# Masked two-precision convolution on TensorE: the four-product form for a second band of rows, with GpSimd in the output path

## What is computed

```python
mask = _predictor_mask(x)                 # mean of 8x8 blocks >= 0.05
x_high = jnp.where(mask, x, EPS)
x_low = jnp.where(mask, EPS, x)
y_high = _conv(_quant_act_uint(x_high, act_scale_high, 8), _quant_weight_per_oc(w_high, 8))
y_low = _conv(_quant_act_uint(x_low, act_scale_low, 4), _quant_weight_per_oc(w_low, 4))
return y_high + y_low
```

## Time and profile before

| | before |
|---|---|
| median of 3 runs | 664.49 us (664.17 to 666.38) |
| the profiled execution: time, and span inside it | 662.33 us, 660.5 us |
| PE busy | 635.5 us (96%), 3714 matmuls |
| DVE busy | 594.5 us (90%), 739 instructions |
| ACT busy | 483.7 us (73%), 491 instructions |
| POOL busy | 10.2 us (2%), 30 instructions |
| granted TensorE clock, mean | 0.996 of full speed |

### The profile page before, as it was taken

How to read it: one execution, slowest core, us unless ns; L and a number is a source line. 1 busy time by engine, 2 the same in 40 slices (tenths; PEclk the granted TensorE clock), 3 DMA queues, 4 the chain that set the end, 5 groups by cost and what they waited for, 6 DMA issues and landing times.

```text
span 660.5 us, 10672 instructions
## 1 busy us (share of the span) xinstructions
PE 635.5 (96%) x3714; PEld 355.9 (54%) x3714; DVE 594.5 (90%) x739; ACT 483.7 (73%) x491; POOL 10.2 (2%) x30
## 2 busy tenths in 40 slices
PE   3779999999999999999999999999999999999996
PEld 1345555555555555555555555555555555555554
DVE  7899999999999999999999999999999999999933
ACT  6768787777777778778777778777877877877442
POOL 3200000000000000000000000000000000000000
PEclk9989999999999999999999999999999999999999
DMA  6245445533435543334543344553343454331122
GB/s 266 97 154 195 162 174 195 194 134 128 182 140 194 194 158 124 163 146 188 194 186 127 132 177 157 194 194 148 122 175 139 194 194 170 124 150 68 72 97 98
DMA packets 14409, 104.07 MB, mean 158 GB/s; under 512 B 1728, under 2 KB 1728, under 8 KB 10432
## 3 DMA queue, kind: packets, MB, share of 16 engines
q1 hardware_dynamic: 14400, 103.95, 41.2%
HBM read 52.56 MB, written 51.38 MB: 157 GB/s over the span
## 4 chain that ended last, share of the span: by engine, by line
PE 95%; ACT 2%; DVE 1%; DMA 1%; issue 0%; DVEq 0%; SPq 0%
PE psum L336 95%; DMA wraw_l<-w_low 1%; ACT rounded_h L450 0%; ACT psum L485 0%; ACT wT_l L467 0%; DVE pooled L619 0%; DVE w_max_l L578 0%; ACT wT_h L467 0%; PE psum L322 0%; DVE ybuf L717 0%; DVEq L63 0%; DVE wq_l L601 0%; DVE wint_l L585 0%; DVE upper L701 0%; DVE wq_l L590 0%
## 5 line engine op out<-in xcount | busy, mean ns | idle before, releaser
L485 ACT ACTIVATE psum<-psum,ratio 128x1344 f32<-128x1344 f32 (+2 forms) x159 | 174.4, 1097 | 131.0 <-PE psum L336 128.3
L336 PE MATMUL psum<-plane_l,wT_l 128*128 128x448 f16 (+1 forms) x1164 | 211.7, 330 | 0.0
L336 PE MATMUL psum<-plane_h,wT_h 128*128 128x448 f16 (+1 forms) x1164 | 209.5, 328 | 0.0
L336 PEld LDWEIGHTS psum<-plane_l,wT_l 128*128 128x128 f16 x1164 | 112.9, 97 | 83.1 <-issue 2.4
L336 PEld LDWEIGHTS psum<-plane_h,wT_h 128*128 128x128 f16 x1164 | 112.0, 96 | 81.3
L717 DVE SCALAR_TENSOR_TENSOR ybuf<-psum,out_scale_h,shared 128x448 f32<-128x448 f32 (+1 forms) x194 | 114.3, 605 | 27.5 <-PE psum L336 20.1
L619 DVE TENSOR_REDUCE pooled<-xbuf 128x49 f32<-128x3136 f32 (+2 forms) x33 | 109.4, 3315 | 0.0
L506 ACT ACTIVATE shared<-psum,bias,out_scale_h 128x448 f32<-128x448 f32 (+1 forms) x128 | 86.2, 674 | 26.4 <-PE psum L336 23.5
L450 ACT ACTIVATE rounded_l<-xbuf,inv_act_l 128x1568 int16<-128x1568 f32 (+1 forms) x64 | 101.7, 1591 | 4.8 <-DMA xbuf<-x 4.8
L450 ACT ACTIVATE rounded_h<-xbuf,inv_act_h 128x1568 int16<-128x1568 f32 (+1 forms) x64 | 101.9, 1594 | 0.0
L336 PE MATMUL psum<-rowsum_l,wT_l 128*128 128x448 f16 (+1 forms) x384 | 86.9, 335 | 2.3 <-ACT wT_l L467 2.3
(11 more groups left out here) (78 smaller groups left out, 340.4 us busy)
## 6 DMA issues: line engine op xcount, KB each, us to landing
xbuf<-x SPq DMA_DIRECT2D x31, 1568.0 KB, 6.5
y<-ybuf SPq DMA_DIRECT2D x32, 896.0 KB, 3.6
y<-ybuf SPq DMA_DIRECT2D x32, 672.0 KB, 3.9
xbuf<-x SPq DMA_DIRECT2D x1, 896.0 KB, 7.9
xbuf<-x SPq DMA_DIRECT2D x1, 672.0 KB, 5.3
wraw_l<-w_low SPq DMA_DIRECT2D x1, 576.0 KB, 4.1
wraw_h<-w_high SPq DMA_DIRECT2D x1, 576.0 KB, 6.2
act_scales<-scales SPq DMA_DIRECT2D x1, 1.0 KB, 1.8
```

The lines of the kernel that those rows point to most:

```text
L336: last = nc.tensor.matmul(out, wT[k][:, mat, :], moving(k, p, band, row, dx), start=(k == "l" and j == 0), stop=(j == len(parts) - 1), ski ...
L485: return nc.scalar.activation(banks, banks, ACT.Identity, scale=ratio[:, 0:1])
```

## The change

`FAST` becomes (1, 3): the second band takes the four-product form too, in 31 of 32 images, with its own `outer` and `inner`. At the output of both fast bands the middle sums leave VectorE. ScalarE copies M2 with scale to a new tile `second` in SBUF, right behind `shared`; GpSimd forms `upper` = `shared` - `second` and `lower` = `shared` + `second`; VectorE waits for each and writes the two rows as before. There is one `second`, one `upper` and one `lower` for both bands. TensorE signals M2 (`s_high_second`) and waits before it next overwrites M2 until `second` has been read. On VectorE the low and high differences of both bands stand before and behind the rows of band 1.

```diff
-    FAST = (3,)
+    FAST = (1, 3)
...
+        second = sb("second", [P, N_MAX], F32)
...
+            def halves(n, band):
+                g = BANDS * n + band
+                pool.wait_ge(s_shared, g + 1)
+                pool.wait_ge(s_second, fast_index(n, band) + 1)
+                if not (early(n) and band == FAST[0]):
+                    pool.wait_ge(s_out, 2 * (g - 2) + 2)
+                for to, op, ready in ((upper, ALU.subtract, s_upper), (lower, ALU.add, s_lower)):
+                    nc.gpsimd.tensor_tensor(to[:, 0:columns(band)], shared[band % 2][:, 0:columns(band)],
+                                            second[:, 0:columns(band)], op).then_inc(ready, 1)
...
                     products("l", p, band, "M1")
+                    if not (early(n) and band == FAST[0]):
+                        pe.wait_ge(s_second, fast_index(n, band))
                     products("l", p, band, "M2").then_inc(s_low_inner, 1)
...
-                    products("h", p, band, "M2")
+                    products("h", p, band, "M2").then_inc(s_high_second, 1)
...
+                if fast(n, band):
+                    act.wait_ge(s_high_second, fast_index(n, band) + 1)
+                    nc.scalar.activation(second[:, 0:columns(band)], psum[:, BANK[band % 2]["M2"], 0:columns(band)],
+                                         ACT.Identity, scale=out_scale["h"][:, 0:1]).then_inc(s_second, 1)
...
-                dve.wait_ge(s_shared, g + 1)
-                dve.wait_ge(s_high, TILES * g + 2)
-                for to, scale, ready in ((upper, neg_out_scale, s_upper), (lower, out_scale["h"], s_lower)):
-                    nc.vector.scalar_tensor_tensor(to[:, 0:columns(band)], tile(band, "M2"), scale[:, 0:1],
-                                                   shared[band % 2][:, 0:columns(band)], ALU.mult, ALU.add
-                                                   ).then_inc(ready, 1)
...
-                out_row(n, p, 1, 0)
                 if ahead > 0:
-                    differences("l", m, mp, 3)
-                out_row(n, p, 1, 1)
+                    for band in FAST:
+                        differences("l", m, mp, band)
+                out_rows(n, p, 1)
                 if ahead > 0:
-                    differences("h", m, mp, 3)
+                    for band in FAST:
+                        differences("h", m, mp, band)
```

More of the change, by code:

```diff
@@ L143, in conv_program @@
         s_diff = {k: sem(f"differences_ready_{k}") for k in "hl"}
+        s_high_second = sem("second_product")
+        s_second = sem("second_ready")
         s_upper = sem("upper_ready")
@@ L312, in _, with body @@
                                     ).then_inc(s_bias, 1)
+            def halves(n, band):
[7 more added lines that the diff above has]
+                                            second[:, 0:columns(band)], op).then_inc(ready, 1)
+            def body(i, p, _):
+                n = 2 * i + p
+                if not first_image(n):
+                    for band in FAST:
+                        halves(n, band)
+            over_images(pool, body)
         @block.tensor
@@ L768, in body @@
                     for k in "lh":
-                        differences(k, m, mp, 3)
+                        for band in FAST:
+                            differences(k, m, mp, band)
                     return
```

## The result

| | before | after |
|---|---|---|
| median of the runs | 664.33 us (662.20 to 666.38, 4 runs) | 709.22 us (707.60 to 709.88, 4 runs) |
| profiled execution | 662.33, span 660.5 | 708.67, span 706.9 |
| period of an image, mean of 29 | 19.52 | 21.06 |

The ratio is 1.069, interval 1.0662 to 1.0717. The granted clock was 0.996 before and 0.991 after. The prediction was 698 in a range of 668 to 740. The direction was right and the size 11 us short; of the two slow mechanisms that it named, not the forecast's but the first rival's took place.

What follows compares the result with a forecast made beforehand. TensorE bounds the kernel before, VectorE after: 18.88 own work + 0.2 + 1.6 of waits = 20.7 us per image, 600.3 over 29 images, +35.9 in all, so 697 profiled and 698 forecast, range 668 to 740.

Steps and rivals of the forecast that it cites:

- the first rival: GpSimd cuts in between two differences and VectorE stands for both additions: period 21.3, 715 to 744 us, chance 0.22.
- TensorE needs less; VectorE becomes the bound: Second band loses 3 of 15 matmuls, low and high: TensorE saves 1.24 us per image, needing 18.33; VectorE needs 18.88.
- VectorE's own work, 18.88: VectorE per image: 18.33 before, less 1.19 for the last band's sums, plus 1.74 for two more pairs of differences.
- ScalarE, and when `second` is ready: Second band's `second` ready 11.2 us after the third band's row 0 starts on VectorE; ScalarE busy about 545 us.
- GpSimd's price, 1.09: One GpSimd addition of 448 elements takes 1.09 us, the middle of estimates 0.64, 1.09 and 1.53.
- VectorE's differences run through and GpSimd starts at 12.49: Second band: GpSimd waits for all four differences, so VectorE's row 1 waits about 1.6 us; chance 0.58.
- the row at 16.03: Start-up row: a 62-element GpSimd operation under two VectorE differences took 0.60, not 0.32, ending 0.11 after the second.
- the first band's wait: VectorE's wait for `shared` of the first band, put at about 0.2 us per image.
- they cost nothing: The last band's middle sums fall under block sums and output rows and cost nothing, up to 1.15 a piece.
- Faster without disturbance: Rival: GpSimd starts at 11.2 undisturbed; period 19.4 at 1.09 per addition, about 655 us at 0.95; chance 0.17.
- No change: Rival: VectorE's gain in spare time and its new waits just cancel, period 19.5; chance 0.03.

Runs made afterwards that it cites:

- the run at 634.51: Changed kernel with block sums split ahead of the second and last bands' rows, differences behind the second band's rows, ScalarE reordered so `second` comes earlier: 634.51 us.
- the run without GpSimd: Kernel before with four products in both bands, VectorE forming all middle sums from PSUM and nothing copied to `second`: 703.27 us, ratio 1.0595.
- the run with two copies: Changed kernel with two copies of 128 columns on ScalarE ahead of the second band's `second`, shifting GpSimd's start by about 0.4 us: 699.92 us.

## Why the prediction was right in sign and wrong in mechanism

- **TensorE needs less; VectorE becomes the bound.** Right. The chain has VectorE in front, TensorE is idle 2.4 us in the image shown (2.3 foretold), and the run at 634.51 shows that it gets by with a period of 18.61 and 18.53 busy, where 18.33 was foretold.
- **VectorE's own work, 18.88.** Too big: 18.52 by the run without GpSimd. Most of the difference is in how were read: an idle time counts from the end of the instruction before, but instructions without a wait start about 0.09 before that end. At the three waits in the earlier trace rows I took own work to run to the end and not to the next possible start, 3 x 0.09 = 0.27. That error was against the change, and it also hid how much a good order would bring.
- **ScalarE, and when `second` is ready.** Right: 11.2 on the clock that starts with the third band's first row. In the image shown that row starts at 305.28 and GpSimd at 316.45, 11.17 later; the differences begin at 316.02, 10.74 (10.75 foretold). ScalarE's total was 526 and not 545 because of how the forecast counted: added up one by one, its instructions take 60.6 us more than before, as foretold (2.05 times 30), but the busy time counts once what overlaps, and the overlap of neighbours grew from 24.8 to 42.8 us.
- **GpSimd's price, 1.09.** Right: an addition is recorded with 1.13, and from the start of an undisturbed `upper` to that of `lower` 1.08 to 1.09 pass.
- **The step that failed: "VectorE's differences run through and GpSimd starts at 12.49".** Of the 30 images in which work for a next image follows, three went that way (`upper` at 83.84, 127.03 and 673.19, lasting 2.61 to 2.65 while all four differences kept 0.64 and 0.40). In the first, VectorE's row 1 begins at 87.63; without a wait it would have begun at 85.97 (85.06 and the 0.32 and 0.59 that the last difference and row 0 take from start to start), so it is 1.66 late, against the 1.6 of the forecast:

```profile
83.84 2.61 POOL L326 TENSOR_TENSOR upper<-shared,second 128x448 f32<-128x448 f32 x1 [9.22 <-ACT second L537]
...
85.06 0.40 DVE L711 TENSOR_TENSOR inner_l<-plane_l 128x480 f16<-128x480 f16 x1
...
87.63 0.68 DVE L731 SCALAR_TENSOR_TENSOR ybuf<-psum,neg_out_scale,lower 128x448 f32<-128x448 f32 x1 [0.47 <-POOL lower L326]
```

  In the other 27 GpSimd got in, as the first rival had it. I had set the row at 16.03 of the earlier trace rows above it: one case with a small operation, and the three images show that such cases exist. A single row was no ground for 0.58 against 0.22.
- **The size nevertheless came near**, because both mechanisms charge VectorE about the same (1.88 stood inside two differences, against a wait of 1.6), and by luck: own work was put 0.36 too high, the first band's wait and the threshold together 0.50 too low. To check, the image of 21.10 us adds up as 18.52 own work + 1.88 held + 0.54 at the first band's row (the 0.45 shown and the 0.09 of overlap; 0.2 was foretold) + 0.16 by which the threshold is held under the last band's additions (the next row starts 0.36 behind it, 0.20 in the run without GpSimd) = 21.10. The forecast had 18.88 + 0.2 + 1.6 = 20.7. Over 29 images, 610.84 against 600.3 gives 10.5 of the 11.7 us by which the profiled execution, 708.67, passed its forecast of 697. The first rival, whose mechanism it was, had been priced at 715 to 744, too high by the same 0.36 of own work and by 2.2 for the two additions instead of 1.88.
- **Last band: "they cost nothing".** Nearly: its additions lie under block sums and output rows and take 1.13, and only the threshold pays, 0.16.
- **Rivals.** Faster without disturbance: refuted, the disturbance is there in every run in which GpSimd's additions meet differences or row sums. It would have been right for another order of the same work. No change: refuted.

The page "SBUF — State Buffer" of the Trainium skill (section "Who interferes with whom") states that a VectorE instruction with two SBUF inputs contends with a GpSimd instruction that reads SBUF, that one with a single SBUF input doesn't outside certain modes, and that the first holds the interface to its end. The runs agree: 1.35 instead of 0.40 for a held difference, 3.41 unchanged for a block sum over two additions.

## What to carry to other kernels

Before giving work to GpSimd, look at what VectorE will run in that very stretch: beside instructions with two SBUF inputs VectorE pays nearly GpSimd's whole time, beside reductions or rows that read PSUM it pays nothing (709 against 634 us for the same operations here). The number of inputs alone isn't a safe guide, as the next section shows. Look for the loss in the mean duration of neighbouring instructions, split by name, since the waits hide it. And when reading own work from a timeline with waits, take start to start from a stretch without them.

## What the runs showed of the hardware

- In 27 of 30 images GpSimd's additions and VectorE's differences exclude each other in turn: of an addition of 1.13 us, 0.93 to 0.95 falls on the one VectorE instruction that comes next; then that instruction runs, and only then GpSimd's next one.
- Two SBUF inputs aren't needed for it. The threshold, with one small f32 input, was held from 0.19 to 0.44. At the start of the kernel before, a one-element GpSimd operation like the one of 0.19 in the earlier trace rows took 0.82 beside a VectorE instruction that reads one tensor and one value per partition, and ended 0.04 after it:

```profile
7.08 0.82 DVE L585 TENSOR_SCALAR wint_l<-wraw_l,w_inv_l 128x1152 int16<-128x1152 f32 x1
...
7.12 0.82 POOL L304 TENSOR_TENSOR out_scale_l<-w_scale_l,act_scales 128x1 f32<-128x1 f32 x1 [0.66 <-DVE w_inv_l L582]
```

Its twin for the high weights began 0.05 behind such an instruction too and took 0.19 all the same, so who goes first is open there as well.

- What draws the line isn't shown. Every VectorE instruction that was held by GpSimd's additions, or held them up, writes 16-bit values (differences, row sums, mask products, threshold); every one that ran beside them unharmed writes f32 (block sums, output rows). No run has two SBUF inputs with an f32 result beside an addition, so the number of inputs and the type are not separated.
- Who goes first at a border isn't settled. GpSimd was kept out over several consecutive VectorE instructions in 3 of 30 images of the changed kernel and in 9 of 30 of the run with two copies, in the latter at an offset at which it got in elsewhere. What decides there stays open.
